# Three queues of the lag-attention loop in another order: the scaling of the values earlier, the weight splits later, the gate product between the taps

## The reference, cut to what matters

```
q, k, v = conv4(silu(x @ Wq)), conv4(silu(x @ Wk)), conv4(silu(x @ Wv))     # causal, one filter per channel
q, k = rotate(q), rotate(k);  q, k = q / |q|, k / |k|
out = sum over s in 0..3:  sum(q * k[t - s]) / sqrt(D) * sigmoid(a[t - s] * b[t]) * v[t - s]
out = out * rsqrt(mean(out^2) + eps) * norm_w * silu(x @ Wz)
x = layernorm(x + out @ Wout)
```

## Time and profile before

| | |
|---|---|
| median of 3 runs | 3158.07 us (3156.15 to 3159.45) |
| profiled execution | 3159.45 us, of which the span from first to last instruction is 3157.6 us |
| mean granted clock of TensorE | 0.973 |
| busy share, PE / DVE / ACT / POOL | 95% / 58% / 37% / 35% |
| the loop of the third layer | from about 925 to 2045 us of the span |

### The profile page before, as it was taken

How to read it: one execution, slowest core, us unless ns; L and a number is a source line. 1 busy time by engine, 2 the same in 40 slices (tenths; PEclk the granted TensorE clock), 3 DMA queues, 4 the chain that set the end, 5 groups by cost and what they waited for, 6 DMA issues and landing times.

```text
span 3157.6 us, 38080 instructions
## 1 busy us (share of the span) xinstructions
PE 2993.2 (95%) x13984; PEld 2482.2 (79%) x13984; DVE 1829.1 (58%) x2654; ACT 1172.4 (37%) x2546; POOL 1091.7 (35%) x742
## 2 busy tenths in 40 slices
PE   6887399999999999999999999899999999999997
PEld 5676388888878888888888888677888888888886
DVE  4566433333368999999999999853222222222225
ACT  4343222222126666666666666521112111121110
POOL 3555223322223444444444444322223222232221
PEclk9888699999999999999999999999999999999998
DMA  3000110100013222232222222311000100001001
GB/s 121 1 1 1 46 40 21 40 21 21 7 62 81 59 68 63 62 83 61 64 67 61 64 77 70 92 41 40 21 21 21 40 21 21 21 21 41 1 1 54
DMA packets 61802, 135.39 MB, mean 43 GB/s; under 512 B 9136, under 2 KB 9520, under 8 KB 60464
## 3 DMA queue, kind: packets, MB, share of 16 engines
q1 hardware_dynamic: 61616, 132.95, 13.8%
HBM read 90.71 MB, written 8.65 MB: 31 GB/s over the span
## 4 chain that ended last, share of the span: by engine, by line
PE 83%; DVE 3%; issue 1%; SPq 0%; ACT 0%; POOL 0%; DMA 0%; POOLq 0%; DVEq 0%; ACTq 0%
PE A L44 6%; PE A L46 6%; PE B L44 6%; PE A L45 6%; PE B L46 6%; PE B L45 6%; PE S L44 5%; PE S L45 5%; PE S L46 5%; PE OP L44 5%; PE OP L46 5%; PE OP L45 5%; PE T L1202 2%; PE S L1186 2%; PE O L1196 2%; PE O L45 1%
## 5 line engine op out<-in xcount | busy, mean ns | idle before, releaser
L736 POOL TENSOR_TENSOR ffn_in_lo<-ffn_inner,ffn_in_hi 128x512 fp32r<-128x512 f32 x192 | 251.2, 1309 | 1112.8 <-ACT ffn_in_hi L732 1112.8
L732 ACT ACTIVATE ffn_in_hi<-ffn_inner 128x512 fp32r<-128x512 f32 x192 | 121.2, 632 | 562.3 <-DVE ffn_inner L748 362.2
L44 PE MATMUL S<-xT_hi,ffn_w_hi 128*128 128x512 f32 x768 | 298.8, 389 | 0.0
L45 PE MATMUL S<-xT_lo,ffn_w_hi 128*128 128x512 f32 x768 | 298.8, 389 | 0.0
L46 PE MATMUL S<-xT_hi,ffn_w_lo 128*128 128x512 f32 x768 | 298.8, 389 | 0.0
L748 DVE TENSOR_TENSOR ffn_inner<-S,ffn_gated 128x512 f32<-128x512 f32 x64 | 44.3, 692 | 291.4 <-PE S L46 284.9
L748 DVE TENSOR_TENSOR ffn_inner<-B,ffn_gated 128x512 f32<-128x512 f32 x64 | 44.3, 691 | 291.3 <-PE B L46 284.0
L1572 POOL TENSOR_TENSOR lag_rnorm<-lag_norm,minus_half 128x8 f32<-128x8 f32 x64 | 105.4, 1647 | 304.2 <-DVE lag_norm L1747 304.2
L44 PE MATMUL B<-xT_hi,lag_w_hi 128*128 128x512 f32 x512 | 206.8, 404 | 0.0
L44 PE MATMUL A<-xT_hi,lag_w_hi 128*128 128x512 f32 x512 | 205.9, 402 | 0.0
L46 PE MATMUL B<-xT_hi,lag_w_lo 128*128 128x512 f32 x512 | 200.6, 392 | 0.0
(11 more groups left out here) (295 smaller groups left out, 8024.0 us busy)
## 6 DMA issues: line engine op xcount, KB each, us to landing
lag_raw<-in_head_weights SPq DMA_DIRECT2D x64, 256.0 KB, 4.5
lag_b_row<-lag_b_scratch SPq DMA_DIRECT2D x64, 256.0 KB, 3.4
lag_rot_q<-lag_r SPq DMA_DIRECT2D x128, 128.0 KB, 2.3
lag_rot_k<-lag_r SPq DMA_DIRECT2D x128, 128.0 KB, 2.3
ffn_raw<-in_expert_gate SPq DMA_DIRECT2D x16, 512.0 KB, 3.6
ffn_raw<-in_expert_up SPq DMA_DIRECT2D x16, 512.0 KB, 4.5
ffn_raw<-in_expert_down SPq DMA_DIRECT2D x16, 512.0 KB, 5.2
x_tok<-in_x SPq DMA_DIRECT2D x4, 1024.0 KB, 5.4
```

The source lines that it names most:

```text
L44: pe.matmul(out, lh, rh, start=first and k == 0, stop=False)
L45: pe.matmul(out, lh, rl, start=False, stop=False)
L732: act.activation(self.in_hi[t % 2][:, f, :], self.inner[f], ACT.Copy).then_inc(self.s_hhi, 1)
L736: pool.tensor_tensor(self.in_lo[t % 2][:, f, :], self.inner[f], f32(self.in_hi[t % 2][:, f, :]), ALU.subtract).then_inc(self.s_hlo, 1)
```

## The change

The order of statements changes in the slots of three queues; no operation and no wait is added, removed or resized.

- ScalarE: `normed_values(l1)` goes from behind c1's copy to directly behind `gates(l1)`, ahead of A's Silu. The split of the next head's (or the experts') weights goes from ahead of A's Silu to behind c1's copy. `mixture(l1)` goes from behind the square of c2 to ahead of it.
- POOL: `r1` goes ahead of the low parts of the split.
- VectorE: `gains` goes from ahead of c1's first tap to behind it, and `probabilities` from behind the third tap to ahead of it.

```
 # ScalarE
                     if l1:
                         gates(l1)
+                        normed_values(l1)
+                    act.wait_ge(s_a1, f.s + 1)
+                    act.activation(A, A, ACT.Silu).then_inc(s_s1, 1)
+                    until(act, s_cos1, f.s)
+                    until(act, s_cross2, f.s)
+                    act.wait_ge(s_s1, f.s + 1)
+                    act.activation(c1, A, ACT.Copy, scale=weight(f, 0, TAPS)).then_inc(s_t1, 1)
                     if f.b and f.head + 1 < HEADS:
...
                         experts.split_hi(act, 0, (f.b - 1,))
-                    act.wait_ge(s_a1, f.s + 1)
-                    act.activation(A, A, ACT.Silu).then_inc(s_s1, 1)
-                    until(act, s_cos1, f.s)
-                    until(act, s_cross2, f.s)
-                    act.wait_ge(s_s1, f.s + 1)
-                    act.activation(c1, A, ACT.Copy, scale=weight(f, 0, TAPS)).then_inc(s_t1, 1)
-                    if l1:
-                        normed_values(l1)
                     act.wait_ge(s_a2, f.s + 1)
...
+                    if l1:
+                        mixture(l1)
                     act.wait_ge(s_c2, f.s * TAPS + TAPS)
                     act.activation(squares[1], c2, ACT.Square).then_inc(s_sqr, 1)
-                    if l1:
-                        mixture(l1)
 # POOL
+                    pool.wait_ge(s_c1, f.s * TAPS + TAPS)
+                    until(pool, s_move1, f.s * 32)
+                    pool.tensor_tensor(r1, c1, cos, ALU.mult).then_inc(s_cos1, 1)
                     if f.b and f.head + 1 < HEADS:
                         split_head(f.head + 1, 1 - f.wbuf, SPLIT_AT[f.b])
                     elif f.b:
                         experts.split_lo(pool, 0, (f.b - 1,))
-                    pool.wait_ge(s_c1, f.s * TAPS + TAPS)
-                    until(pool, s_move1, f.s * 32)
-                    pool.tensor_tensor(r1, c1, cos, ALU.mult).then_inc(s_cos1, 1)
 # VectorE
+                    dve.wait_ge(s_t1, f.s + 1)
+                    tap(0, f, A, c1, 1, s_c1)
                     if l1:
                         gains(l1)
-                    dve.wait_ge(s_t1, f.s + 1)
-                    tap(0, f, A, c1, 1, s_c1)
                     tap(0, f, A, c1, 2, s_c1)
-                    tap(0, f, A, c1, 3, s_c1)
                     if l1:
                         probabilities(l1)
+                    tap(0, f, A, c1, 3, s_c1)
```

## The result

The changed kernel takes 3204.28 us (median of 4 runs, 3202.77 to 3204.78) against 3157.11 us; the ratio is 1.0148, with an interval of 1.0131 to 1.0166. That is 47 us more; the forecast was 3197, 39 more. Its profiled execution took 3204.01 us, with a span of 3202.1.

The account below looks back on a forecast made before the run. TensorE bounds the kernel at 16.99 us a slot. 15 heads add 33.6 us, the last head 5.4, less about 1: 3158.1 + 38 = 3196, stated as 3197; own range 3183 to 3212, chance 0.68.

Parts of the forecast that it names:

- Step 1: ScalarE's values, ahead of A's Silu, wait for POOL's root: c1's first tap L + 4.19, against L + 2.72.
- L: The end of the slot's norm on VectorE (line L1747), from which the slot's times in us are counted.
- Steps 2 and 3: VectorE's new order lets v start at L + 7.50; the v path puts cv's first tap at L + 11.87.
- The first ring: Loop of norm, POOL's root, values, c1, v, cv, next norm: 17.33 us without a split, against TensorE's 16.99.
- One way is longer by 0.34: In slots without a split the next norm ends at L + 17.33, that is +0.34 us.
- Step 4: ScalarE's mixed copy ahead of c2's square: VectorE starts cross1 before POOL's sum, 0.60 us instead of 1.66, saving 1.06.
- Step 6: Later splits meet VectorE's products: +0.76 us (b=1, 2), +0.38 (b=3), +1.7 per split slot in the last head.
- The port: Rival: VectorE can't get in between POOL's two subtractions; 1.3 us more in 30 slots, 3236 us; chance 0.13.
- Nothing: Rival: the way from norm to cv is 0.34 us shorter than added up, time stays 3158; chance 0.08.
- faster: Rival: TensorE sets the pace and gets 9 us back as neighbours move, 3149 us; chance 0.06.
- The clock: Rival: TensorE's short waits lower its clock for six matmuls each, 94 us more, 3290 us; chance 0.05.
- What the profile after would show: Signs: TensorE about 96.5% busy, waits ahead of v; ScalarE idles about 0.9 us, VectorE 2.4 before c1's first tap.

Follow-up runs that it names:

- e10: The kernel before with only the mixed copy moved ahead of c2's square: 3158.63 us, ratio 1.0001.
- e7: The kernel before with only the probabilities moved ahead of c1's third tap: 3180.73 us, ratio 1.0070.
- e1: The changed kernel with only the scaled values moved back behind c1's copy: 3194.53 us, ratio 1.0112.
- e3: The changed kernel, nothing undone, plus VectorE's norm ahead of the gated output and ScalarE's high part of y behind the gates: 3195.66 us, ratio 1.0115.
- e12: The changed kernel with only gains moved back ahead of c1's first tap: 3193.69 us, ratio 1.0105.
- e5: The changed kernel with only the probabilities moved back behind c1's third tap: 3173.69 us, ratio 1.0047.
- e4: The changed kernel with only the mixed copy moved back behind c2's square: 3227.57 us, ratio 1.0214.
- e9: The changed kernel with only POOL's order undone, the split's subtractions ahead of r1 again: 3239.11 us, ratio 1.0253.
- e8: The kernel before with only the scaled values moved directly behind the gates, ahead of the splits and A's Silu: 3210.91 us, ratio 1.0165.

## Why the prediction was right, and where it was not

**What bounds the kernel.** Right: TensorE sets the 16.99 us of the kernel before, and VectorE's 97% was no second bound. e10 takes 30 us per 500 off VectorE's busy time and changes nothing.

**Step 1, the root pulled ahead of c1.** Right in kind and nearly in size: first tap at L + 4.28 us against 4.19. The values took 1.02 to the next start, Silu to copy 0.72, copy to tap 0.73, each a little above the row I took.

**Steps 2 and 3, the way to v and back.** Third tap's end L + 7.56 against 7.45, v L + 7.62 against 7.50, cv's first tap L + 12.05 against 11.87, the next norm L + 17.50 against 17.33. Half of the missing 0.17 was there at the first tap, the rest came in the taps and in TensorE's restart. The four slots add 2.64 us to a head, against 2.24 in the sum; over 15 heads that is 6 of the 8 us between forecast and result.

**The step that was missing.** Step 2 priced the probabilities at 0.60 us of VectorE's queue and did not ask what they wait for. Put ahead of the third tap, they tie v to the scores of the same slot on TensorE, and that ring, scores - probabilities - third tap - v, takes more than 16.99 us by itself. e7 shows it alone (+21 us), e1, e3 and e12 show it left over (+33 to +36 us, with what the later splits add to it). The first ring, over the root, shows in e5 (+14 us), where the probabilities no longer lengthen it; some 10 of these lie in the 30 slots with two subtractions. The changed kernel has both, and their prices don't add up: its probabilities start 0.08 us behind the scores without a wait on them in the list, so the first ring is the longer one there, and the second lies just beneath it. So the forecast came near with a cause that is only half of the story. "One way is longer by 0.34" was right for the first ring, which does set the changed kernel's slot. But undoing the early values gives back 10 us, not the 47 that I expected of e1. That the unpriced tie did not spoil the number was luck: in the changed kernel the probabilities start 0.08 us behind the end of the scores, and in e1 and e7, where they wait for them, 0.04 us. A first ring shorter by a little would have left the time with the tie.

**Step 4, the exchange of the mixed copy and the square.** Right: cross1 0.68 us at b = 0, and e4 gives the price of undoing it, 23 us (I had worked out 17 at least).

**Step 6, the splits.** cross2 at 1.29 us, hidden; b = 1 and 2 17.79 against 17.75, b = 3 17.52 against 17.37, the last head 18.56 against 18.7. Right as sums, and cross1 meets r2 as it was worked out: it ends L + 13.68 against 13.64 in the slot with b = 1 that follows 1236.70. The gain that I listed, gains at 0.69 instead of 1.72, was of no use, since gains no longer stood in a wait. e9 shows the other side: r1 ahead of the split was what kept POOL away from gains.

**The rivals.** The port did not cost more: VectorE got in between two subtractions, as in the earlier trace rows. "Nothing" and "faster" failed with the ring above 16.99. The clock stayed at 1.00 from 1000 to 1900 us, with a wait in each slot. It fell once in the first slots: TensorE waited 3.07 us up to 944.72, and the granted clock of 945 to 950 us was 0.66, where it was 1.00 before, behind a wait of 2.79. e10 has the same wait of 3.07 us, 0.71 in that stretch, and the time of the kernel before.

**What the profile after would show.** The waits and the times of the single instructions came as listed. TensorE's busy share did not: 98.7% against the 96.5% forecast, with the count of matmuls down to 96.3% instead.

## What to carry to other kernels

Before moving an operation up in a queue, write down what it waits for, not only what it takes: what stands behind it inherits that wait, and so does the engine that waits for those. When a cause is found, undo it alone and see whether the time comes back; if it does not, another bound is close behind, and several different repairs that stop at one and the same time are its mark. A fall of an engine's busy share is no gain unless that engine sets the pace, and a short wait of TensorE is seen in the number of matmuls per stretch before it is seen in its busy share.

## What the runs showed of the hardware that I had not expected

The price of meeting POOL is decided within hundredths of a microsecond: with POOL's sum 0.10 us ahead cross1 took 1.74 us, with 0.02 us 1.82, and with 0.01 us or less it mostly took 0.68 and the sum 1.81 to 1.86 (e4, e8). And VectorE's busy time counts that wait, so a kernel with 56 us less of it per 500 was the slower one.
